# A graph-attention and mixture-of-experts kernel: b2 in bfloat16 parts, row numbers kept by copies, four pieces of work in other places

## The reference, cut to what matters

```python
for t in range(4):                                # graph attention, all batches
    q, k, v = products of [x_loc, xc, pl * pc]
    prob = softmax(where(adj > 0, leaky(edge_score), -9e15))
    x_ctx = lin(concat([xc, prob @ v]), w_mu)
y = lin(concat([x_loc, x_ctx]), w_cb)
y = layernorm1(y + mha(y))                        # 16 heads
e, weight = best expert of the best group, g_prob * e_prob   # of 8
moe = weight * (relu(y @ w1[e] + b1[e]) @ w2[e] + b2[e])     # per token
out = x + layernorm2(y + moe)
```

## Time and profile before

| what | us |
|---|---|
| median of 3 runs (533.24, 534.62, 534.55) | 534.55 |
| the profiled execution's own time | 533.24 |
| its span in the profile | 531.3 |
| PE busy (share of the span) | 482.1 (91%) |
| DVE busy | 425.7 (80%) |
| ACT busy | 380.8 (72%) |
| GpSimd busy | 272.5 (51%) |

### The profile page before, as it was taken

The page is one execution under the profiler, slowest core; times in us unless marked ns, Lnnn a source line. Parts: engine busy times, 40 slices in busy tenths (PEclk is TensorE's granted clock), DMA queues, the critical chain, the costliest instruction groups (busy, mean ns, idle before and its releaser), DMA issues. The chain is left out here.

```text
span 531.3 us, 14967 instructions
## 1 busy us (share of the span) xinstructions
PE 482.1 (91%) x4945; PEld 331.7 (62%) x4945; DVE 425.7 (80%) x1190; ACT 380.8 (72%) x1151; POOL 272.5 (51%) x462
## 2 busy tenths in 40 slices
PE   5998889999999999999978999999999878789990
PEld 3765556667776767766534565656565545689990
DVE  2489988888888888999864568888888887898992
ACT  3567688888887888777844767768687754678990
POOL 0485763332222223303623445678788756577774
PEclk9999999999999999999998999999999998989996
DMA  8800799999999200040420000001104113525530
GB/s 345 336 1 2 230 296 300 290 295 283 307 297 301 69 0 0 22 138 1 163 76 2 3 1 2 12 23 51 43 33 182 41 51 100 144 86 146 150 108 10
DMA packets 49955, 65.65 MB, mean 124 GB/s; under 512 B 2509, under 2 KB 45522, under 8 KB 48736
## 3 DMA queue, kind: packets, MB, share of 16 engines
q1 hardware_dynamic: 47104, 58.42, 37.7%
q0 software_dynamic: 2784, 6.37, 3.4%
HBM read 21.04 MB, written 44.19 MB: 123 GB/s over the span
## 5 line engine op out<-in xcount | busy, mean ns | idle before, releaser
L1605 DVE TENSOR_REDUCE nm<-SC 128x8 f32<-128x1024 f32 x64 | 75.4, 1219 | 30.1 <-PE SC L1099 29.4
L2120 ACT ACTIVATE room_p<-ST 128x512 f32<-128x512 f32 (+1 forms) x96 | 64.1, 739 | 37.5 <-PE ST L1118 37.5
L1501 DVE TENSOR_REDUCE room_w<-SC 128x512 f32<-128x2048 f32 x32 | 73.0, 2281 | 1.0 <-PE SC L928 1.0
L600 POOL TENSOR_TENSOR spread<-parts,units 128x48 bf16<-128x48 bf16 x32 | 8.8, 275 | 124.5 <-DVE parts L1476 124.5
L2027 ACT ACTIVATE room_w<-room_w,shift 128x128 f32<-128x128 f32 x128 | 49.7, 390 | 19.4 <-DVE shift L1510 19.4
L2018 ACT ACTIVATE room_w<-ST,cv 128x128 f32<-128x128 f32 x128 | 36.4, 365 | 18.4 <-PE ST L943 18.4
L795 POOL DMA_INDIRECT out<-room_v x39 | 38.2, 981 | 12.5 <-issue 8.2
L701 POOL DMA_INDIRECT sorted_rows<-room_w,slot_i x32 | 33.4, 1042 | 17.7 <-issue 9.3
L943 PEld LDWEIGHTS ST<-room_w 128*128 128x128 f32 x256 | 33.1, 191 | 14.2 <-issue 13.0
L1112 PE MATMUL ST<-room_v,room_w 32*128 32x512 f32 x256 | 37.3, 651 | 4.8 <-DVE room_w L1629 1.9
L2036 ACT ACTIVATE room_w<-room_w,inv 128x128 f32<-128x128 f32 x128 | 41.0, 407 | 0.1
(11 more groups left out here) (302 smaller groups left out, 1330.7 us busy)
## 6 DMA issues: line engine op xcount, KB each, us to landing
sorted_rows<-w SPq DMA_DIRECT2D x8, 4290.0 KB, 38.2
room_v<-sorted_rows SPq DMA_DIRECT2D x39, 130.0 KB
x_t<-xT SPq DMA_DIRECT2D x2, 1024.0 KB, 8.3
ctx_t<-adj SPq DMA_DIRECT2D x1, 2048.0 KB, 16.9
biased_rows<-room_w SPq DMA_DIRECT2D x2, 1024.0 KB, 4.3
room_w<-biased_rows SPq DMA_DIRECT2D x8, 256.0 KB
room_w<-mask SPq DMA_DIRECT2D x1, 1536.0 KB, 19.8
w<-weights SPq DMA_DIRECT2D x1, 1356.0 KB, 8.9
```

The lines of the kernel that those rows point to most:

```text
L1501: dve.tensor_reduce(logit[:, :, :], SC[:, :, :].rearrange("p b (i m) -> p b m i", i=TYPES), AX_X, ALU.max)\
L1605: dve.tensor_reduce(nm[:, v % 2, 2 * PER_R * pair:2 * PER_R * (pair + 1)], SC[:, 2 * pair:2 * pair + 2, :].rearrange("p r (i n) -> p (r i) ...
L2120: act.activation(ex[:, v % 2, first:last, :], ST[:, first:last, :], ACT.Exp)\
```

## The change

**b2.** Before, one DMA spreads b2 over 128 partitions, in the middle of SyncE's program. Now SyncE loads it at the start as 8 rows of 128; GpSimd splits it into three bfloat16 parts (`bias_parts`, five chained instructions on 8 partitions, behind `add_bias(3)`); SyncE writes these to DRAM and reads them back as three rows of 1024. The parts lie in the place of `prob_t` for that time, so ACT's first `probabilities_out` waits for the write (`b2_moved` at 16). The bias product on PE becomes one of three bfloat16 rows with ones.

**Row numbers.** GpSimd copies the row numbers of each tile into `id_r`, one tile ahead of the output; the output reads them there. A tile's place may be loaded again when its number is kept and `fin` is ready, without the output having landed.

**Fillers.** `warm` becomes a bfloat16 product of 512 columns in place of a float32 one of 128.

**Places.** `first_taken` goes from step 29 to step 31; `rows_x1` of group 6 from DVE (k = 2) to GpSimd (k = 1); `rows_x1` and the later links of group 7 from k = 4 to k = 5; the last `residual` on PE from behind the turn of tile 1 to k = 2, behind the rank products of group 6.

```diff
+            sp.dma_start(b2_s, b2.rearrange("o (e d) -> (o e) d", e=EXPERTS)).then_inc(in_rest, 16)
             sp.dma_start(id_s[:, :], ids).then_inc(in_rest, 16)
+            sp.wait_ge(S("b2_parts"), 5)
+            sp.dma_start(b2_rows.rearrange("n (e d) -> e n d", e=EXPERTS), b2_p).then_inc(S("b2_moved"), 16)
+            sp.wait_ge(S("b2_moved"), 16)
+            sp.dma_start(b2_h, b2_rows).then_inc(S("b2_moved"), 16)
...
-            sp.dma_start(b2_all, b2.broadcast_to([128, EXPERTS * D])).then_inc(S("in_b2"), 16)
...
                     sp.wait_ge(S("fin_ready"), k - RING + 1)
-                    sp.wait_ge(S(f"sent{(k - RING) % OUTS}"), turn_of(k - RING, OUTS))
+                    sp.wait_ge(S("id_kept"), k - RING + 1)
...
+            def bias_parts():
+                pool.wait_ge(in_rest, 48)
+                pool.tensor_copy(b2_p[:, 0, :], b2_s).then_inc(S("b2_parts"), 1)
+                for n in range(1, NPART):
+                    pool.wait_ge(S("b2_parts"), 2 * n - 1)
+                    pool.tensor_tensor(b2_s, b2_s, b2_p[:, n - 1, :], ALU.subtract).then_inc(S("b2_parts"), 1)
+                    pool.wait_ge(S("b2_parts"), 2 * n)
+                    pool.tensor_copy(b2_p[:, n, :], b2_s).then_inc(S("b2_parts"), 1)
...
             add_bias(3)
+            bias_parts()
...
                 if k == 1:
                     norm1_power(G - 1)
+                    rows_x1(G - 2)
...
                 rest(k)
+                t = k - LAST + 1
+                if 0 <= t < SLOTS:
+                    pool.wait_ge(S(f"in_tile{t % RING}"), turn_of(t, RING))
+                    if t >= RING:
+                        pool.wait_ge(S(f"sent{(t - RING) % OUTS}"), turn_of(t - RING, OUTS)).then_inc(S("passed"), 1)
+                    pool.tensor_copy(id_r[:, t % RING:t % RING + 1],
+                                     tile_s[:, t % RING, 2 * D + 1:2 * D + 2].bitcast(I32)).then_inc(S("id_kept"), 1)
                 t = k - LAST
                 if t >= 0:
-                    pool.wait_ge(S(f"in_tile{t % RING}"), turn_of(t, RING))
+                    pool.wait_ge(S("id_kept"), t + 1)
                     pool.wait_ge(S("fin_ready"), t + 1).then_inc(S("passed"), 1)
...
-                    pe.matmul(bank[:, 0:D], C("before"), C("ones"), start=True, stop=True)
+                    pe.matmul(four(bank), before_h[:, :], ones_h[:, :].unsqueeze(1).broadcast_to([128, 4, N]),
+                              start=True, stop=True)
...
+                if k == 2:
+                    pe.wait_ge(S("h_ready"), B - 1)
+                    residual(B - 1)
...
-                    pe.matmul(YB[t % 2], C("ident")[:, 0:1].broadcast_to([128, N]), b2_all[:, bass.ds(e * D, D)],
-                              start=True, stop=False)
+                    pe.matmul(YB[t % 2], ones_h[0:NPART, :], b2_h[:, bass.ds(e * D, D)], start=True, stop=False)
...
                 if k == 1:
-                    pe.wait_ge(S("h_ready"), B - 1)
-                    residual(B - 1)
                     ranks(k)
...
-                if u == B - 3:
-                    first_taken()
...
+                if u == B - 1:
+                    first_taken()
...
                     route(G - 2, range(12, SLOT_LINK))
-                    rows_x1(G - 2)
...
                     route(G - 1, range(7, 12))
+                if k == 5:
                     rows_x1(G - 1)
                     route(G - 1, range(12, SLOT_LINK))
...
             def probabilities_out(s):
                 act.wait_ge(pt_done, s + 1)
+                if isinstance(s, int) and s == 0:
+                    act.wait_ge(S("b2_moved"), 16)
```

More of the change, by code:

```diff
@@ L116, in build @@
     biased_rows = nc.dram_tensor("biased_rows", (N, B, D), F32, kind="Internal").ap()
+    b2_rows = nc.dram_tensor("b2_rows", (NPART, EXPERTS * D), BF16, kind="Internal").ap()
     with ExitStack() as ctx:
@@ L183, in build @@
         prob = A(128, GB, N)
+        b2_at = used["a"]
         prob_t = A(128, GB, N)
@@ L282, in build @@
         w1_s = x_t[:, 0:EXPERTS * W1ROW]
+        b2_s = room_w[0:EXPERTS, b2_at:b2_at + D]
+        b2_p = room_w[0:EXPERTS, b2_at + D:b2_at + D + NPART * D // 2].bitcast(BF16).rearrange("p (n d) -> p n d", n=NPART)
         init_row, init_all, key_first, query_first = (ctx_raw[:, n * D:(n + 1) * D] for n in range(4))
@@ L299, in build @@
         eps_s = sb("eps_s", [128, 1])
+        id_r = sb("id_r", [128, RING], I32)
         base_h = sb("base_h", [128, EXPERTS], BF16)
@@ L789, in _ @@
                 rest(k)
+                t = k - LAST + 1
[5 more added lines that the diff above has]
+                                     tile_s[:, t % RING, 2 * D + 1:2 * D + 2].bitcast(I32)).then_inc(S("id_kept"), 1)
                 t = k - LAST
                 if t >= 0:
-                    pool.wait_ge(S(f"in_tile{t % RING}"), turn_of(t, RING))
+                    pool.wait_ge(S("id_kept"), t + 1)
                     pool.wait_ge(S("fin_ready"), t + 1).then_inc(S("passed"), 1)
-                    number = tile_s[:, t % RING, 2 * D + 1:2 * D + 2].bitcast(I32)
-                    pool.indirect_dma_start(out, bass.IndirectOffsetOnAxis(ap=number, axis=0),
+                    pool.indirect_dma_start(out, bass.IndirectOffsetOnAxis(ap=id_r[:, t % RING:t % RING + 1], axis=0),
                                             fin[:, t % OUTS, :], None, bounds_check=TOK - 1, oob_is_err=False)\
@@ L1012, in _ @@
             local(7)
-            pe.wait_ge(in_rest, 32)
+            pe.wait_ge(in_rest, 48)
             v_product(2, 2)
```

9 lines of the change are left out of this document (4 added, 5 removed).

## The result

Over eight runs of each the median is 537.61 us after (534.97 to 539.24) and 533.52 before (531.46 to 534.62). The ratio is 1.0061, with a 95% interval of 1.0038 to 1.0084: the change makes the kernel 2 to 4.5 us slower. That ratio is of more executions than the eight: the record lists sixteen of the changed kernel, with a median of 536.28. The profiled execution of the changed kernel took 535.78 with a span of 534.0, that of before 533.24 with 531.3, so the two traces differ by 2.7 us. Here is where they lie, each stage measured between the starts of instructions that both kernels have ("row maximum" is DVE's `neg_top`, "statistics" its `stats`).

What follows compares the result with a forecast made beforehand. GpSimd's queue was taken as the bound from its first output on. Terms 0.8 + 0.5 + 0.3 + 1.25 = +2.85 on 533.24 gave 536.1; half the distance to the median added made 536.8 us, range 532.8 to 540.

Steps and rivals of the forecast that it cites:

- Bound: Expert loop and end: GpSimd's queue sets the pace from its first output on, period 1.28 us at best.
- `first_taken`, -1.85: Before the scatters: moving it to step 31 starts PE's batch 31 earlier at full clock, -1.85 us; -0.6 if the clock falls.
- no window of 0.50 would follow: Behind batch 31: PE's idle time falls to 0.4 us and no window of clock 0.5 comes behind it.
- Residual behind the ranks, +1.0: Before the scatters: DVE stands idle for the last `residual`, so everything behind is 1.0 us later; bounds 0.5 and 1.1.
- `rows_x1` on GpSimd: Group 6's wide adds behind group 7's power: two adds with their link 2.6 us; first scatter +0.5 for three edits together.
- First scatter to first output, +0.3: GpSimd's stretch before the loop: group 6 takes 6.4 us, group 7 6.0, together 12.4 against 12.06; between 0 and +0.8.
- b2 at the start, +0.8: First rounds: ACT waits for the parts' write, landing in 2.5 us; DVE's inverse 2.0 late, partly regained; net +0.8.
- The saving of 1.3 from a missed collision: Start: a later DVE cast, 1.13 us at 57.70, misses GpSimd's wide work, giving 1.3 us back.
- The loop, +1.25: Output loop: each copy adds 0.05 to 0.06 us; 38 periods of 1.335 make 50.7 against 49.48.
- The 0.95 of slack no longer shows: Output loop: the 0.95 us above 38 periods of 1.277 vanishes once the copies lengthen the period.
- PE's tile falls to some 1.05: Expert loop: the bfloat16 bias saves one of eleven PE instructions a tile, bringing 1.20 us to some 1.05.
- Blocked copies: Rival in the output loop: DVE's two-input instructions hold copies 0.1 us in the mean, 3.9 more, 540.5 us; chance 0.1.

Runs made afterwards that it cites:

- experiment 4: The kernel before with `first_taken` alone moved from step 29 to step 31 of DVE; 532.95 us, ratio 0.9972.
- experiment 1: The changed kernel without the copies of row numbers: outputs read them from the tile, loads wait for the landed output; 533.58 us, ratio 1.0003.
- experiment 7: The changed kernel with the last residual on PE again ahead of the rank products; 535.50 us, ratio 1.0048.
- experiment 12: The changed kernel with `rows_x1` of group 6 on DVE again, in its old place; 535.58 us, ratio 1.0051.
- experiment 2: The kernel before with the copies of row numbers alone added; 536.80 us, ratio 1.0055.
- experiment 11: The changed kernel without copies, bias over 128 rows, own rooms for b2's parts, residual early, wide adds ahead of the power, group 7's rows loaded earlier; 530.49 us.
- experiment 3: The changed kernel with copies made but not used: outputs read the tile, loads wait for both events; 536.18 us, ratio 1.0040.
- experiment 5: The kernel of experiment 1 with its bias product as one bfloat16 matmul over 128 rows of constants; 532.18 us, ratio 0.9989.
- experiment 9: The changed kernel, copies kept, with its bias product over 128 rows, zeros filling the weights; 536.01 us, ratio 1.0074.
- experiment 6: The kernel of experiment 1 with its bias product as one float32 product of 3 rows of constants; 589.96 us, ratio 1.1058.

## Why the prediction was right, and where it was not

The forecast was 536.8 with a range of 532.8 to 540, slower as the likeliest; 537.61 came (536.28 over all sixteen executions). By its own steps:

- **Bound.** GpSimd sets the loop and the end: right for the kernel before, although PE's tile there is 1.225 and not the 1.20 that was read from the window. For the changed one it is GpSimd and PE together, at 1.335 and 1.355.
- **`first_taken`, -1.85.** Alone it gave -1.85 at the first scatter and -2.08 at the first output, with the idle time at 0.44 and the clock kept in the window 447, as said. That no window of 0.50 would follow was wrong: one stands at 456 in experiment 4 and at 457 in the changed kernel. It cost the approach nothing that shows: experiment 1, whose clock fell only at 464, has the first scatter 28.74 behind batch 24, the changed kernel 28.77.
- **Residual behind the ranks, +1.0.** 0.99 (experiment 7), by the mechanism named.
- **`rows_x1` on GpSimd.** 0.97 (experiment 12). The prediction did not price it by itself; it had the first scatter at +0.5 for all three edits. Against batch 24 that scatter is +0.30.
- **First scatter to first output, +0.3.** 12.50 for 12.06, so +0.44. The two parts came as 6.41 (462.27 to 468.68) and 6.09 (to 474.77), forecast 6.4 and 6.0; the copies' part of it, by experiments 1 and 2, is 0.75 to 0.77. Approach in sum: +0.8 forecast, +0.74 measured.
- **b2 at the start, +0.8.** The step was mis-sized in its parts: the write of 6 KB released ACT 1.4 us after the parts were done and not 2.5, and DVE was 0.47 late and not 2.0. The saving of 1.3 from a missed collision didn't come either (1.14 at 57.98). The rounds take 216.22 to 216.24 in the six executions where ACT doesn't wait (experiment 11 is one of them), and with the wait 216.57 to 216.62 in five and 216.96 to 216.99 in three. So the term is +0.35 or +0.75. With the wait PE idles 1.13 us until ACT's copy, near 51 us, and in experiments 3, 5 and 7, the three, the granted clock stands at 0.50 from 52 to 54; in the other five, and in the six without the wait, it does not fall there. So the wait is worth 0.35, and the other 0.4 goes with the clock.
- **The loop, +1.25 for +2.65: too small by more than half.** Two things failed. "The 0.95 of slack no longer shows": it does. The minimum pitch rose from 1.277 to 1.335 as forecast, which is 2.2 over 38, but the pitches above the minimum did not vanish. With copies and a quick PE (experiment 9), 52.22 is 1.5 over 38 x 1.335; without copies six loops lie between 49.25 and 50.53, 0.7 to 2.0 over 38 x 1.277. The slack was not free time in which the copies could hide. It was single long DMAs, slower early tiles (PE's first ones, with their fillers, take 1.57 in the changed kernel) and waits that come on top of any pitch; how it divides among them was not taken apart.
- **"PE's tile falls to some 1.05": wrong in sign.** It rose to 1.355. It did no harm to the sum only because the copies stand beside it: alone, the copies brought the loop to 52.57 and PE's tile to 50.91, and together they bring 52.13, no more.
- **Blocked copies.** Their mean is 0.21, under the 0.24 from which that rival was to decide (its 540.5 should be 540.7, 536.8 and 3.9). But its mechanism is in the traces, at some copies (35 in all kernels together) and at the DMA itself: the outputs that take 1.10 for 0.98 are those that start just behind one of DVE's two-input instructions (54 of 61, see experiment 2). It costs 0.12 each time, so 0.4 in the changed kernel's three and 1.3 in the eleven of experiment 2. The prediction's doubt, that the trace does not bear the Trainium skill's rule out for the copies, holds for the copy of 0.19 that it looked at and not for the loop as a whole.

What I had not forecast is the -0.74 between the rounds and the attention batches, where the change touches nothing. It goes with the clock, and the last section tells of it. So +0.4 too much at the start, 1.4 too little in the loop, and 0.7 in the middle and 0.35 at the two ends unseen, leave a total of +2.7 in the profile for +2.85: the sign and the approach were argued rightly, and the closeness of the sum is partly luck.

## What to carry to other kernels

Before an instruction is put into the gap of the engine that bounds a loop, count it at least at the full rise of the smallest pitch times the number of turns, and don't set the loop's other losses against it: here they stayed. A smaller matmul is not a cheaper one; look in the trace whether its weights are loaded under the matmul ahead, and fill up the rows with zeros if they aren't. That pays only where PE sets the pace: 1.66 us of loop without the copies, nothing with them. Take a change of many edits apart on the approach between two fixed instructions: four edits worth -2.1, +1.0, +1.0 and +0.8 looked like one of +0.7.

## What the hardware showed that I had not expected

**A weight load of three rows is not overlapped.** It costs 0.24 us a tile against a product over 128 rows (1.355 to 1.11), in every kernel with three rows of bfloat16 (the changed one, experiments 1, 3, 7 and 12), and float32 shows the same order of loads (experiment 6). The load itself takes the same 0.09 to 0.10 for 3 rows and for 128.

**A DMA's start beside a two-input instruction of DVE.** An indirect DMA that begins 0.05 to 0.11 us behind such an instruction takes 1.05 to 1.12 on GpSimd for 0.98 (54 of 61 in the fourteen traces).

**The same clock fall, or none, at the same place.** At the turn from the rounds to the attention batches PE idles for 1.30 us in every kernel, and some 6 us later for 1.3 again, or for 0.4 to 0.9 where the clock has fallen in between. Windows of PE of before, then of after:

```profile
279.00:280.00 1.00, 1.00 (x7) 0.65 0.00 0
280.00:281.00 1.00, 1.00 (x16) 0.50 0.00 0
```

```profile
275.00:276.00 1.00, 1.00 (x24) 0.73 0.00 0
276.00:277.00 1.00, 1.00 (x8) 0.50 0.00 0
```

Before, the clock fell to 0.50 (1.2 GHz) from 279 on, after the second idle time; in the changed kernel from 275, after the first, as in five others; and in seven executions, experiments 1 and 9 among them, not at all. The stretch from the last row maximum to the first statistics takes 44.58, 43.8 to 44.1, and 42.9 to 43.0 us in these three cases. The kernels are alike there, so up to 1.7 us of any two profiles can be this, and it is a reason to compare stages and not ends.

**A clock that stays down under a busy PE,** in experiment 6: 0.50 for over 100 us with PE busy all the time.
